# Attention with block-diagonal values as stationary operand: probabilities streamed, no transposes of the heads

## The reference

```
HD = 16; NH = 16                      # heads of 16 channels
h = layernorm(x)                      # scale and bias per channel
q, k, v = h @ w_qkv + b_qkv           # cross: q from layernorm(x), k and v from ctx
scores = einsum('bhqd,bhkd->bhqk', q, k) / sqrt(HD)
scores = scores * mask - 10000 * (1 - mask)
probs = softmax(scores)               # over 64 keys
x = x + merge_heads(einsum('bhqk,bhkd->bhqd', probs, v)) @ w_o + b_o
...
x = x + mlp(layernorm(x)); x = recurrent_block(x, state from ctx)
```

## Time and profile before

| | |
|---|---|
| median of 3 runs | 1130.16 us (1126.83 to 1130.65) |
| profiled execution | 1127.48 us, span 1125.7 us |
| TensorE matmuls | 1067.1 us busy, 95% of the span, 12992 records |
| TensorE weight loads | 898.8 us, 80% |
| VectorE | 914.3 us, 81% |
| ScalarE | 705.7 us, 63% |
| GpSimd | 591.5 us, 53% |
| mean granted TensorE clock | 0.988 |
| chain that ended last | TensorE 83%, VectorE 9%, issue 4%, ScalarE 3% |

### The profile page before, as it was taken

One profiled execution on the slowest core, in us unless ns is written; L12 is line 12 of the kernel. 1 busy time (PEld: TensorE's weight loads), 2 busy tenths in 40 slices (PEclk: granted clock), 3 DMA queues, 4 the chain that ended last, 5 costly groups with the idle time before them and its releaser, 6 DMA issues.

```text
span 1125.7 us, 34405 instructions
## 1 busy us (share of the span) xinstructions
PE 1067.1 (95%) x12992; PEld 898.8 (80%) x12992; DVE 914.3 (81%) x1677; ACT 705.7 (63%) x1606; POOL 591.5 (53%) x520
## 2 busy tenths in 40 slices
PE   5899999999999998999999999999999997887798
PEld 4889889888988987778778888778888776665677
DVE  5987777888777775129999999999999999899864
ACT  4778788777877875555545565546555545535574
POOL 4787878878788784034443444443444343433121
PEclk9999999999999998999999999999999999889999
DMA  9500000011111110022233332133332123304011
GB/s 331 167 4 2 0 0 3 3 40 47 44 37 46 38 38 2 1 59 68 54 75 85 85 85 60 35 75 84 84 84 61 34 74 85 84 2 120 20 38 57
DMA packets 39868, 65.01 MB, mean 58 GB/s; under 512 B 4385, under 2 KB 26209, under 8 KB 39393
## 3 DMA queue, kind: packets, MB, share of 16 engines
q1 hardware_dynamic: 39776, 63.75, 21.3%
HBM read 55.35 MB, written 8.39 MB: 57 GB/s over the span
## 4 chain that ended last, share of the span: by engine, by line
PE 83%; DVE 9%; issue 4%; ACT 3%; POOL 1%; DMA 0%; DVEq 0%; ACTq 0%; POOLq 0%
PE psum L982 10%; PE psum L353 10%; PE psum L991 9%; PE psum L1071 9%; PE psum L267 5%; PE psum L336 5%; PE psum L368 5%; PE psum L297 4%; PE psum L280 3%; PE psum L1031 3%; PE psum L1109 2%; PE psum L1251 2%; PE psum L310 2%; PE psum L1142 2%; DVE shared L1763 2%
## 5 line engine op out<-in xcount | busy, mean ns | idle before, releaser
L1763 DVE TENSOR_TENSOR_SCAN shared<-late_wT,shared 128x512 f32<-128x512 f32 x128 | 175.6, 1372 | 0.0
L892 POOL TENSOR_TENSOR late_xm<-late_mixed,late_xa 128x512 f32<-128x512 f32 x64 | 91.4, 1438 | 106.2 <-DVE late_mixed L1729 106.1
L232 POOL TENSOR_TENSOR shared<-shared,att_row_max 128x512 f32<-128x512 f32 x128 | 132.5, 1054 | 17.3 <-DVE att_row_max L564 17.3
L353 PE MATMUL psum<-shared 128*128 128x128 f32 x1024 | 126.7, 277 | 0.0
L453 ACT ACTIVATE shared<-shared 128x512 f32<-128x512 f32 x128 | 80.5, 631 | 67.5 <-POOL shared L232 67.4
L982 PE MATMUL psum<-late_glnT,w 128*128 128x256 f32 x512 | 119.8, 387 | 1.8 <-ACT late_glnT L1359 1.8
L353 PEld LDWEIGHTS psum<-shared 128*128 128x128 f32 x1024 | 121.0, 194 | 0.2 <-ACT shared L462 0.2
L564 DVE TENSOR_REDUCE att_row_max<-shared 128x8 f32<-128x512 f32 x128 | 86.8, 679 | 41.0 <-POOL shared L225 40.9
L991 PE MATMUL psum<-w,late_hT 128*128 128x256 f32 x512 | 118.6, 380 | 1.0 <-ACT late_hT L1368 0.9
L901 POOL TENSOR_TENSOR shared<-shared,late_rT 128x512 f32<-128x512 f32 x32 | 40.8, 1274 | 143.0 <-DVE shared L1763 143.0
L982 PEld LDWEIGHTS psum<-late_glnT,w 128*128 128x128 f32 x512 | 95.8, 192 | 18.0 <-issue 2.8
(11 more groups left out here) (167 smaller groups left out, 2433.7 us busy)
## 6 DMA issues: line engine op xcount, KB each, us to landing
shared<-v_rows SPq DMA_DIRECT2D x64, 512.0 KB, 7.3
shared<-in_enc SPq DMA_DIRECT2D x64, 128.0 KB, 2.6
v_rows<-shared SPq DMA_DIRECT2D x64, 64.0 KB, 1.8
out<-x SPq DMA_DIRECT2D x16, 256.0 KB, 2.0
x<-in_x SPq DMA_DIRECT2D x7, 512.0 KB, 9.8
w<-in_w SPq DMA_DIRECT2D x2, 1024.0 KB, 17.3
shared<-in_cross_mask SPq DMA_DIRECT2D x1, 1024.0 KB, 12.3
shared<-in_w_qkv SPq DMA_DIRECT2D x1, 768.0 KB, 4.8
```

What stands on the lines that cost most here:

```text
L232: nc.gpsimd.tensor_tensor(zs, zs, peak.unsqueeze(2).to_broadcast([P, PAIRS, S]), ALU.subtract).then_inc(shifted, 1)
L353: last = nc.tensor.matmul(dst[:, half * P:(half + 1) * P], w[:, kb, c0 + half * P:c0 + (half + 1) * P], src[:, u % 2, kb, 0:P], start=(kb ...
L892: nc.gpsimd.tensor_tensor(xm[m % XM].rearrange("p h (b t) -> p (h b) t", t=S), mixed[:, m % 2, :, :].rearrange("p h (b t) -> p (h b) t", t=S),
L1763: nc.vector.tensor_tensor_scan(states, wT[:, u, half, :, :, :].rearrange("p j b t -> p (j b t)"), states, 0.0, ALU.mult, ALU.add).then_inc ...
```

## The change

`attend` swaps the operands. The values of a pair of heads are laid out block-diagonally: 64 keys of the even head by its 16 channels, 64 keys of the odd head by its 16 channels, zeros elsewhere, a stationary operand of 128 rows and 32 columns. The transposed probabilities of the pair are streamed, 64 columns for a sequence. The result has channels on partitions, as the output projection needs it, so the transposes of the heads go. Four matmuls with a block-diagonal operand of ones give each head's sums, repeated over its 16 partitions: `recip` grows from 128x16 to 128x256. V is projected in halves of 64 rows, even heads to partitions 0 to 63, odd heads to 64 to 127; the input and the context are no longer kept twice side by side, and the context is loaded once. V shares its bank with the transposed input, and `project_v` moves behind `project_out`; on ScalarE, `copy_heads` moves ahead of `copy_ln`, and `copy_values` behind `copy_q`, as two instructions. `project_v`'s waits for weights and for the context move to `project_qk`.

```
-    lnT = core.shared[:, 10240:11264].rearrange("p (a b c) -> p a b c", b=2, c=256)
+    lnT = core.shared[:, 10240:10752].rearrange("p (a b c) -> p a b c", b=2, c=P)
...
-    recip = sb("recip", [P, NH])
+    recip = core.shared[:, 18768:19024]
+    head_ones = core.shared[:, 17936:17936 + 2 * HD]
...
-    tr, hh = core.banks[4][:, 0:C], core.banks[4][:, C:2 * C]
-    vv = core.banks[5][:, 0:C]
+    outs, sums = core.banks[5][:, 0:C], core.banks[5][:, C:2 * C]
+    tr, vv = core.banks[4][:, 0:C], core.banks[4][:, C:2 * C]
...
-            for copy in range(2):
-                sp.dma_start(encT[:, u % 2, :, copy * P:(copy + 1) * P],
-                             core.dram["enc"][:, :, ds(t, P)]).then_inc(enc_loaded, 16)
+            sp.dma_start(encT[:, u % 2, :, :], core.dram["enc"][:, :, ds(t, P)]).then_inc(enc_loaded, 16)
...
             pe.wait_ge(probsT_copied, HALVES * (n + 1))
-            pe.wait_ge(v_copied, n + 4 if there(*on(k, t, 3)) else ALL)
-            pe.wait_ge(ln_ready, n + 5 if there(*on(k, t, 4)) else ALL)
+            pe.wait_ge(v_copied, n + 1)
             if later(n):
-                pe.wait_ge(headsT_copied, n)
+                pe.wait_ge(heads_ready, n)
             pe.nop(nofuse=True)
-            for pair in range(PAIRS):
-                for e in range(2):
-                    keys = slice(e * S, (e + 1) * S)
-                    for b in range(BPT):
-                        rows = slice(b * S, (b + 1) * S)
-                        last = nc.tensor.matmul(out_banks[e ^ b][rows, pair * 32:pair * 32 + HD + 1], zT[keys, pair, rows],
-                                                values[keys, u, e ^ b, pair, :], start=True, stop=True)
+            for half in range(HALVES):
+                for b in range(BPT):
+                    cols = slice(b * S, (b + 1) * S)
+                    for g in range(4):
+                        pair = 4 * half + g
+                        nc.tensor.matmul(outs[32 * g:32 * (g + 1), half * P + b * S:half * P + (b + 1) * S],
+                                         values[u][:, b, pair, :], zT[:, pair, cols], start=True, stop=True)
+            for g in range(4):
+                last = nc.tensor.matmul(sums[32 * g:32 * (g + 1), :].rearrange("p (h t) -> p h t", t=P),
+                                        head_ones[:, :], zT[:, g::4, :], start=True, stop=True)
             last.then_inc(out_ready, 1)
...
             pe.wait_ge(xn_ready, n + 1)
-            if later(n - 4):
-                pe.wait_ge(heads_ready, n - 4)
+            if later(n - 1):
+                pe.wait_ge(v_copied, n - 1)
...
-        def transpose_heads(k, t):
-            n = k * TILES + t
-            pe.wait_ge(heads_ready, n + 1)
-            for half in range(HALVES):
-                last = nc.tensor.transpose(hh[:, half * P:(half + 1) * P], heads[:, half * P:(half + 1) * P],
-                                           core.ident[:, :])
-            last.then_inc(headsT_ready, 1)
-
         def project_v(k, t, u):
             n = k * TILES + t
             wv, v0 = WV[k]
+            pe.wait_ge(ln_ready, n + 2 if there(*on(k, t, 1)) else ALL)
+            if later(n):
+                pe.wait_ge(v_copied, n)
+            for b in range(BPT):
+                for kb in range(HALVES):
+                    for e in range(2):
+                        last = nc.tensor.matmul(
+                            vv[e * S:(e + 1) * S, b * P:(b + 1) * P].rearrange("p (r d) -> p r d", d=HD),
+                            KV[k][:, u % 2, kb, b * S:(b + 1) * S],
+                            wv[:, kb, v0:v0 + C].rearrange("p (r e d) -> p r e d", e=2, d=HD)[:, :, e, :],
+                            start=(kb == 0), stop=(kb == HALVES - 1))
+            last.then_inc(v_ready, 1)
...
-            if there(k, t):
-                transpose_heads(k, t)
             if there(*on(k, t, 4)):
-                project_v(*on(k, t, 4), u + 4)
                 project_qk(*on(k, t, 4), u + 4)
             if there(k, t):
                 project_out(k, t)
+            if there(*on(k, t, 4)):
+                project_v(*on(k, t, 4), u + 4)
...
-                last = nc.scalar.activation(lnT[:, u % 2, half, :].rearrange("p (n t) -> p n t", t=P),
-                                            tr[:, half * P:(half + 1) * P].unsqueeze(1).to_broadcast([P, 2, P]),
+                last = nc.scalar.activation(lnT[:, u % 2, half, :], tr[:, half * P:(half + 1) * P],
...
-            nc.scalar.activation(values[:, u, :, :, 0:HD].rearrange("p b r d -> p (b r) d"),
-                                 vv.rearrange("p (n d) -> p n d", d=HD), ACT.Copy).then_inc(v_copied, 1)
+            for e in range(2):
+                keys = slice(e * S, (e + 1) * S)
+                last = nc.scalar.activation(values[u][keys, :, :, e * HD:(e + 1) * HD].rearrange("p b r d -> p (b r) d"),
+                                            vv[keys, :].rearrange("p (n d) -> p n d", d=HD), ACT.Copy)
+            last.then_inc(v_copied, 1)
...
-            nc.vector.reciprocal(recip[:, :].rearrange("p (e r) -> p e r", e=2),
-                                 outs[:, :, :, HD]).then_inc(recip_ready, 1)
+            nc.vector.reciprocal(recip[:, :], sums).then_inc(recip_ready, 1)
             dve.wait_ge(recip_ready, n + 1)
             if later(n):
-                dve.wait_ge(headsT_ready, n)
-            nc.vector.tensor_tensor(
-                heads[:, :].rearrange("p (r e d) -> p e r d", e=2, d=HD), outs[:, :, :, 0:HD],
-                recip[:, :].rearrange("p (e r) -> p e r", e=2).unsqueeze(3).to_broadcast([P, 2, PAIRS, HD]),
-                ALU.mult).then_inc(heads_ready, 1)
+                dve.wait_ge(headsT_copied, n)
+            nc.vector.tensor_tensor(heads[:, :], outs, recip[:, :], ALU.mult).then_inc(heads_ready, 1)
```

More of the change, by code:

```diff
@@ L244, in gpsimd_part @@
         nc.gpsimd.memset(core.eps[:, :], EPS).then_inc(eps_set, 1)
-        nc.gpsimd.memset(core.values[:, :, :, :, :], 1.0).then_inc(core.ones_set, 1)
+        for u in range(4):
+            nc.gpsimd.memset(values[u].rearrange("p b r d -> p (b r d)"), 0.0).then_inc(core.ones_set, 1)
+        nc.gpsimd.memset(head_ones[:, :], 0.0).then_inc(core.ones_set, 1)
+        for e in range(2):
+            pool.wait_ge(core.ones_set, 5 + e)
+            nc.gpsimd.memset(head_ones[e * S:(e + 1) * S, e * HD:(e + 1) * HD], 1.0).then_inc(core.ones_set, 1)
+        pool.wait_ge(core.ones_set, 7)
         nc.gpsimd.memset(core.maa_w2b[:, :, :], 0.0).then_inc(zeroed, 1)
@@ L330, in project_v @@
             if k:
-                pe.wait_ge(enc_loaded, 32 * t + 32)
-            if later(n):
-                pe.wait_ge(v_copied, n)
-            for e in range(2):
-                for kb in range(HALVES):
-                    last = nc.tensor.matmul(
-                        vv[:, e * P:(e + 1) * P].rearrange("p (r d) -> p r d", d=HD),
-                        KV[k][:, u % 2, kb, e * S:e * S + P],
-                        wv[:, kb, v0:v0 + C].rearrange("p (r e d) -> p r e d", e=2, d=HD)[:, :, e, :],
-                        start=(kb == 0), stop=(kb == HALVES - 1))
-            last.then_inc(v_ready, 1)
-        def project_qk(k, t, u):
-            n = k * TILES + t
+                pe.wait_ge(enc_loaded, 16 * t + 16)
             if later(n - 2):
@@ L470, in copy_heads @@
             for half in range(HALVES):
-                last = nc.scalar.activation(headsT[:, half, :], hh[:, half * P:(half + 1) * P], ACT.Identity,
+                last = nc.scalar.activation(headsT[:, half, :], heads[:, half * P:(half + 1) * P], ACT.Identity,
                                             bias=col(core, B_V[k], half))
@@ L480, in body @@
                 copy_probs(*on(k, t, 1))
+            if there(k, t):
+                copy_heads(k, t)
             if there(*on(k, t, 5)):
                 copy_ln(*on(k, t, 5), u + 5)
-            if there(k, t):
-                copy_heads(k, t)
-            if there(*on(k, t, 4)):
-                copy_values(*on(k, t, 4), u % 4)
             if there(*on(k, t, 6)):
@@ L959, in _ @@
         def _(pe):
-            attend, transpose_probs, transpose_heads, attention_out = att.tensor(pe)
+            attend, transpose_probs, attention_out = att.tensor(pe)
             def mlp_transpose(g):
@@ L1298, in _ @@
             mlp_transpose(0)
-            transpose_heads(1, end - 2)
             up(0, 0)
@@ L1305, in _ @@
             up(0, 2)
-            transpose_heads(1, end - 1)
             up(0, 3)
@@ L1312, in _ @@
             down(0, 2)
-            transpose_heads(1, end)
             down(0, 3)
```

31 lines of the change are left out of this document (16 added, 15 removed).

## The result

| | before | after |
|---|---|---|
| median of 4 runs | 1130.22 us (1126.83 to 1130.65) | 1185.26 us (1184.41 to 1186.9) |
| profiled execution, span | 1127.48, 1125.7 us | 1186.9, 1185.1 us |
| TensorE matmuls | 1067.1 us, 95%, 12992 records | 1079.8 us, 91%, 11840 records |
| VectorE / ScalarE / GpSimd | 914.3 / 705.7 / 591.5 us | 1005.6 / 733.4 / 592.4 us |
| mean granted TensorE clock | 0.988 | 0.980 |

The change costs 5.0%: ratio 1.0496, interval 1.0472 to 1.0519. The forecast was 1172 us; the time lies inside its range (1144 to 1222), 13 us above the forecast.

The account below looks back on a forecast made before the run. TensorE alone was taken to bound the kernel before, at 6.45 us a period. Both loops rise to 7.06: 64 periods x 0.61 = 39 us, plus 5 for longer periods, on 1127.5 gives 1172 us, range 1144 to 1222.

Parts of the forecast that it names:

- main case: Whole kernel: 7.06 us a period with the reciprocal at 1.48 us, so 1160 to 1185 us; chance 0.52.
- loop B: VectorE and GpSimd, mask through row maxima, residual and division to next mask: 5.82 us before, forecast 7.06.
- TensorE's sum: All of TensorE's own work in one attention period: 6.34 us forecast, 0.11 less than 6.45.
- rival 3: Counted among the slower outcomes; the prediction as given does not spell out its claim, size or chance.
- The reciprocal, the mis-sized term: VectorE's division step: reciprocal of 256 sums instead of 16 forecast at 1.48 us, 1.24 more than before.
- rival 1: Reciprocal costs as much an element as other operations, 0.49 us; 6.80 us a period, 1150 us; chance 0.20.
- rival 2: Reciprocal is dearer, 8.6 ns an element, 2.3 us; 7.87 us a period, 1222 us; no chance given.
- V moved: V behind the output projection: 0.35 us a period lost in front of Q and K; V's copies costed at nothing.
- the two loops: loop A, over ScalarE, and loop B, over VectorE and GpSimd; both forecast at 7.06 us a period.
- Rival 4: Faster: TensorE stays the bound and gains its 0.11 us a period, 7 us in all, 1120 us; chance 0.10.
- loop A: Mask through GpSimd, row maxima, ScalarE's exponentials and probability copies to Q and K, over two periods; forecast 7.06 us a period.
- The periods that were longer already: Some eight periods with statistics and norms on VectorE pay the whole 1.24 us, 0.63 more each, 5 us.

Follow-up runs that it names:

- experiment 1: Changed kernel with a plain copy of the sums in place of their reciprocal; 1162.72 us, ratio 1.0326.
- experiment 2: Changed kernel with V put back ahead of Q and K and the input's transposes moved behind them; 1173.22 us, ratio 1.0405.
- experiment 3: Changed kernel with both a copy in place of the reciprocal and V back ahead of Q and K; 1126.91 us, ratio 0.9996.
- experiment 6: Kernel of experiment 1 with V copied out of PSUM by VectorE, no longer by ScalarE; 1156.16 us, ratio 1.0258.
- experiment 5: Changed kernel with the two transposes of the input done four times over, filling TensorE's idle time; 1180.36 us, ratio 1.0473.
- experiment 7: Kernel of experiment 2 with the multiplication by the reciprocal moved behind the mask on VectorE; 1168.14 us, ratio 1.0357.
- experiment 8: Kernel of experiment 7 with the copy of V ahead of the copy of the heads on ScalarE; 1143.88 us, ratio 1.0146.
- experiment 4: Kernel before the change, with only the reciprocal widened to 256 elements a row; 1222.07 us, ratio 1.0834.

## Why the prediction was right, and where it was off

**Direction and main case.** Slower, at 7.06 us a period; measured 7.12 in self attention and 7.22 in cross attention. TensorE idles in front of Q and K, the mask comes straight behind the division, both as forecast. By experiments 1 and 2, cross attention is held by loop B, as forecast, with a dearer reciprocal, and self attention by loop C, which the forecast did not have. The step from ScalarE's end to TensorE's start is 0.10 us here, not 0.15.

**TensorE's sum.** Attend 1.03, V 1.03, all together 6.34. Measured 1.01, 1.02 and, in experiment 3, 6.37, so the prices of the earlier trace rows held. The 64-column matmuls on 32-column tiles pack (8 rounds in 0.47 us, that is 0.059 each), so rival 3 is out. The warning of the Trainium skill, "TensorEngine Tiling (Array Packing)", Key Properties, that a change of the tiling mode drains TensorE, shows at most in the slots and hardly in the sum. In experiment 3, where Q and K follow V's 64-column tiles, they take 1.89 us to the next group's start (117.21 to 119.10) against 1.78 behind a group of their own shape; the transposes that follow gain 0.06, and the sum, with a fifth shape in the period, is 0.03 above the forecast.

**The reciprocal, the mis-sized term.** "(249 - 167)/16 = 5.1 ns an element ... 1.48 us": it is 1.75. Two points of the same operation, 16 and 256 elements, give (1750 - 249)/240 = 6.25 ns an element and 149 ns fixed. I had taken the fixed part of another operation, 18 ns too much, and dividing by 16 and multiplying by 256 made 0.27 us of it. Rivals 1 (0.49) and 2 (2.3) are out. The fixed part of 167 ns was not one that every VectorE row has, as the prediction says: operations on 128x4 in the kernel before take 151 ns (L529).
**V moved.** "V's end is the period's end, and the second exponential is due later (T+1.66), so I cost it at nothing": this step failed. Both exponentials queue behind the copies of V, and the copies of the probabilities behind them, which closes loop C at 7.11 us. Experiments 1 and 6 show it. The forecast came out near anyway, in self attention by luck: loop C's 7.11 and the two loops' 7.06 happen to be alike. Had the reciprocal been cheap, my rival 1 (1150, 6.80 a period) would have been wrong by some 13 us; experiment 1 measured that case at 1162.7. Rival 4 needed a loop A that is shorter by 0.9 us and a cheap reciprocal; experiment 3, which has a cheap one and the cover back, reaches no more than the time of before.

**The periods that were longer already.** "Some eight periods are longer already ...; they pay the whole 1.24, 0.63 more each, 5 us." The 63 distances grew by 60.9 us: 35.5 in the ordinary ones, where 48 x 0.61 = 29 was expected, and 25.4 in the 15 others, where 15 x 0.61 + 5 = 14 was. So of a miss of some 15 us against the profiled execution, 6 come from the period and 11 from the others, less 1.5 for an earlier start. In those others VectorE pays 1.5 us, not 1.24, and TensorE's granted clock fell in some: five took 9.84 to 10.49 us, and experiment 5 gives back 1.5 to 1.6 us in each of four, over 6 us; the first distance grew by 3.4 us at a mean clock of 0.72. Nothing in the prediction allowed for a lower granted clock where TensorE idles longer.

## What to carry to other kernels

Before an instruction is widened to save a step elsewhere, price it by two sizes of its own row or keep both ends open: an operation that costs little at 16 elements (249 ns) may be the most expensive one at 256. Before a step is moved to the end of a period, follow what consumes it on every in-order queue, and what stands behind that consumer: here the copy of V, two entries further on, held up Q and K, and in experiments 7 and 8 the order of two entries in ScalarE's list was worth 24 us. Count the loops that close within one period as well as those that close over two; where several have the same length, taking one away shows nothing, and only the experiment that takes both (3) tells what they cost.

## What the hardware showed

- VectorE's reciprocal costs 6.25 ns an element beside 149 ns fixed (249 ns at 16, 1750 ns at 256 elements a partition, fp32 from PSUM), while the multiplication of the same size takes 424 ns and the copy that replaced it 422.
- TensorE's granted clock fell from 2.4 to 1.2 GHz in some periods with an idle stretch of only 1.45 us before Q and K, and Q and K then took 3.65 instead of 2.02 us. The period ahead of it had the same 1.45 us of idle time and kept its clock, so the length of that stretch alone doesn't decide; what does, stays open here. In experiment 4, with 1.12 us idle in nearly every period, ten of the ordinary ones took 9.2 instead of 7.6 us, at a mean clock of 0.82. In experiment 2 the long periods idle longer in all (0.83, 0.25 and 0.66 us in that from 72.78 to 81.08), and those of self attention keep their clock.
- Q and K's slot is 1.78 us where they follow directly behind matmuls of their own shape, 1.86 behind an idle stretch (387.55 to 389.41) and 1.89 behind another tile shape (experiment 3). So a group that starts afresh, for either reason, took about 0.1 us more here.
